# Products of low weights over the last 64 features, two at a time in half of the rows each

## The reference

```python
x = normalized_resid_pre                                   # [64, 36, 192]
q = jnp.einsum('bsd,hde->bshe', x, W_Q) + b_Q              # 12 heads of 64
k = jnp.einsum('bsd,hde->bshe', x, W_K) + b_K
v = jnp.einsum('bsd,hde->bshe', x, W_V) + b_V
scores = jnp.einsum('bqhe,bkhe->bhqk', q, k) / math.sqrt(D_HEAD)   # causal mask
pattern = jax.nn.softmax(scores, axis=-1)
z = jnp.einsum('bhqk,bkhe->bqhe', pattern, v)
attn_out = jnp.einsum('bqhe,hed->bqd', z, W_O) + b_O
```

## Time and profile before

| | |
|---|---|
| median of 3 runs | 899.01 us (897.86 to 900.95) |
| profiled execution, its time | 903.05 us |
| its span | 901.3 us |
| PE busy | 818.9 us (91%) |
| PEld busy | 733.5 us (81%) |
| DVE busy | 542.0 us (60%) |
| ACT busy | 439.9 us (49%) |
| POOL busy | 408.7 us (45%) |

### The profile page before, as it was taken

How to read it: one execution, slowest core, us unless ns; L and a number is a source line. 1 busy time by engine, 2 the same in 40 slices (tenths; PEclk the granted TensorE clock), 3 DMA queues, 4 the chain that set the end, 5 groups by cost and what they waited for, 6 DMA issues and landing times. The chain is left out here.

```text
span 901.3 us, 21350 instructions
## 1 busy us (share of the span) xinstructions
PE 818.9 (91%) x7767; PEld 733.5 (81%) x7767; DVE 542.0 (60%) x1467; ACT 439.9 (49%) x1094; POOL 408.7 (45%) x489
## 2 busy tenths in 40 slices
PE   9899999999998898987999989888879999999973
PEld 8889998899997676766999976666657899899973
DVE  2235565556665898993763337788966622467645
ACT  0246555555644576763345527566626221355523
POOL 1534444344444544342442236767841455244444
PEclk9999999999999999996999989898979999999996
DMA  9910111111110232225200013623200111333252
GB/s 308 265 51 21 31 27 37 31 32 30 37 37 2 35 67 26 34 22 172 24 1 1 1 27 50 157 47 65 46 3 2 36 60 63 81 99 107 77 170 94
DMA packets 103942, 55.78 MB, mean 62 GB/s; under 512 B 67264, under 2 KB 94512, under 8 KB 103840
## 3 DMA queue, kind: packets, MB, share of 16 engines
q1 hardware_dynamic: 99248, 45.99, 21.2%
q0 software_dynamic: 3792, 7.84, 2.5%
q10 hardware_dynamic: 800, 0.59, 0.2%
HBM read 29.81 MB, written 13.97 MB: 49 GB/s over the span
## 5 line engine op out<-in xcount | busy, mean ns | idle before, releaser
L931 POOL TENSOR_TENSOR attn_prob<-attn_prob,attn_recip 100x432 f32<-100x432 f32 x64 | 58.6, 916 | 67.1 <-DVE attn_recip L1316 66.6
L450 POOL TENSOR_TENSOR attn_prob_x<-attn_prob,attn_recip 100x864 f32<-100x864 f32 x32 | 52.6, 1644 | 52.8 <-DVE attn_recip L759 52.8
L1892 POOL DMA_INDIRECT results<-moe_hid_shared x43 | 41.1, 955 | 58.1 <-ACT moe_hid_shared L2107 58.1
L1602 ACT ACTIVATE mlp_hid<-psum,columns 128x384 f32<-128x384 f32 x72 | 38.1, 580 | 41.4 <-PE psum L96 41.4
L1047 PE MATMUL psum<-ident,attn_prob 100*108 100x100 f32 x256 | 35.5, 264 | 21.4 <-POOL attn_prob L931 12.9
L1047 PEld LDWEIGHTS psum<-ident,attn_prob 100*108 100x108 f32 x256 | 26.1, 138 | 27.2 <-POOL attn_prob L931 18.7
L1064 PEld LDWEIGHTS psum<-attn_prob_t,attn_values 108*49 108x49 f32 (+1 forms) x1024 | 33.7, 132 | 15.5 <-ACT attn_prob_t L1183 6.7
L1176 ACT ACTIVATE attn_prob<-attn_prob 100x432 f32<-100x432 f32 x64 | 36.1, 564 | 19.0 <-POOL attn_prob L938 17.8
L2082 ACT ACTIVATE moe_silu<-psum 128x384 f32<-128x384 f32 x36 | 17.7, 491 | 56.5 <-PE psum L107 56.5
L1064 PE MATMUL psum<-attn_prob_t,attn_values 108*49 108x36 f32 (+1 forms) x1024 | 36.0, 217 | 8.3 <-DMA attn_values<-attn_v_tok 5.0
L1555 PE MATMUL psum<-mlp_w_dn_s,mlp_hid 128*128 128x192 f32 (+2 forms) x306 | 42.6, 290 | 0.0
(11 more groups left out here) (474 smaller groups left out, 2790.5 us busy)
## 6 DMA issues: line engine op xcount, KB each, us to landing
embed_patches<-in_x SPq DMA_DIRECT2D x8, 768.0 KB, 14.5
sorted_rows<-mlp_pad_zeros SPq DMA_DIRECT2D x1, 4214.0 KB, 15.6
moe_hid_shared<-sorted_rows SPq DMA_DIRECT2D x43, 98.0 KB, 2.1
attn_v<-attn_v_tok SPq DMA_DIRECT2D x16, 216.0 KB
attn_values<-attn_v_tok SPq DMA_DIRECT2D x96, 27.0 KB
side_raw_a<-in_w_gu_dram SPq DMA_DIRECT2D x8, 288.0 KB, 3.2
side_raw_b<-in_w_gu_dram SPq DMA_DIRECT2D x16, 144.0 KB, 3.4
h_rows<-results SPq DMA_DIRECT2D x6, 288.0 KB, 5.4
```

The costliest lines, as they stand in the source:

```text
L450: nc.gpsimd.tensor_tensor(prob_x[k % 2][:, :, :, :], prob[k % 3][:, :, :].rearrange("p h (a n) -> p h a n", a=1) .to_broadcast([QP, HEADS, ...
L931: nc.gpsimd.tensor_tensor(pr, pr, recip[k % 2][:, :].rearrange("p (h a) -> p h a", a=1) .to_broadcast([QP, HEADS, SEQ]), ALU.mult).then_in ...
L1602: nc.scalar.activation(hid_step(n), bank(n % 3)[:, 0:MW], ACT.Gelu, bias=b_up[:, c:c + 1]).then_inc(S["gelu_done"], 1)
L1892: nc.gpsimd.indirect_dma_start(out=results, out_offset=bass.IndirectOffsetOnAxis(ap=x_in[j % x_ring][:, D:D + 1].bitcast(U32), axis=0), in ...
```

## The change

The low products of the last 64 features need only 64 rows, w_lo and x_hi. The change computes them in pairs: the query chunk's product in the upper half of the rows, the key chunk's in the lower half, and for values the left 384 columns above and the right 384 below. For the lower half x_hi must lie in partitions 64 to 127 as well, which a new tile `b_upper` holds, written by a third rounding on ACT for each group. `project` now makes queries and keys in one call: it waits for all three copies of the chunk two before, does four matmuls for the queries, four for the keys, and then the pair. `values` does four and four, and then the pair. The low weights of the first attention are subtracted over all 128 partitions, so three of four memsets fall away. What the diff takes from `part_views` and `width` is a view that was unused.

```diff
+        if self.b_upper is not None:
+            nc.scalar.activation(self.b_upper[DB:P, 0:MW], self.x_b, ACT.Copy).then_inc(S["next_rounded"], 1)
     def split(self, dve, S):
-        dve.wait_ge(S["next_rounded"], 2)
+        dve.wait_ge(S["next_rounded"], 2 if self.b_upper is None else 3)
...
-            def project(g, kind, c):
+            def project(g, c):
                 if c == 0 and g >= 1:
                     pe.wait_ge(S["x_split"], g)
-                if c >= 2 and kind == 0:
+                if c >= 2:
                     pe.wait_ge(S["q_copied"], chunks * g + c - 1)
-                elif c >= 2:
                     pe.wait_ge(S["k_low_copied"], chunks * g + c - 1)
                     pe.wait_ge(S["k_high_copied"], chunks * g + c - 1)
...
+                cols, toks = slice(c * P, (c + 1) * P), group_cols(g)
+                for w, out in ((w_q, q_bank(c)), (w_k, k_bank(c))):
+                    nc.tensor.matmul(out, w.a_hi[:, cols], a_hi[:, toks], start=True, stop=False)
+                    nc.tensor.matmul(out, w.a_hi[:, cols], a_lo[:, toks], start=False, stop=False)
+                    nc.tensor.matmul(out, w.a_lo[:, cols], a_hi[:, toks], start=False, stop=False)
+                    nc.tensor.matmul(out, w.b_hi[:, cols], b_x[:, toks], start=False, stop=False)
+                nc.tensor.matmul(q_bank(c), w_q.b_lo[0:DB, cols], b_x[0:DB, toks], start=False, stop=True
+                                 ).then_inc(S["q_done"], 1)
+                nc.tensor.matmul(k_bank(c), w_k.b_lo[DB:P, cols], b_upper[DB:P, toks], start=False, stop=True
+                                 ).then_inc(S["k_done"], 1)
...
                     nc.tensor.matmul(out, b_x[:, toks], w_v.b_hi[:, cols], start=False, stop=False)
-                    nc.tensor.matmul(out, b_x[:, toks], w_v.b_lo[:, cols], start=False, stop=True
-                                     ).then_inc(S["v_done"], 1)
+                nc.tensor.matmul(bank(0)[:, 0:half], b_x[0:DB, toks], w_v.b_lo[0:DB, 0:half], start=False, stop=True
+                                 ).then_inc(S["v_done"], 1)
+                nc.tensor.matmul(bank(1)[:, 0:half], b_upper[DB:P, toks], w_v.b_lo[DB:P, half:HID],
+                                 start=False, stop=True).then_inc(S["v_done"], 1)
...
                 nc.scalar.activation(b_x[0:DB, at], bank(1)[0:DB, 0:n], ACT.Copy).then_inc(S["x_rounded"], 1)
+                nc.scalar.activation(b_upper[DB:P, at], bank(1)[0:DB, 0:n], ACT.Copy).then_inc(S["x_rounded"], 1)
...
-                dve.wait_ge(S["x_rounded"], 2 * g)
+                dve.wait_ge(S["x_rounded"], 3 * g)
...
-                    for w in (w_q1, w_k1, w_v1, w_qkv2_split):
-                        nc.gpsimd.memset(w.b_lo[DB:P, :].bitcast(F32), 0.0).then_inc(S["pads_cleared"], 1)
+                    nc.gpsimd.memset(w_qkv2_split.b_lo[DB:P, :].bitcast(F32), 0.0).then_inc(S["pads_cleared"], 1)
```

More of the change, by code:

```diff
@@ L198, with __init__ @@
 class FirstTokens:
-    def __init__(self, nc, psum, ident, neg_half, rows_, x, banks, ready, norm=None, room=None):
+    def __init__(self, nc, psum, ident, neg_half, rows_, x, banks, ready, norm=None, room=None, b_upper=None):
         self.nc, self.ident, self.neg_half, self.rows, self.ready, self.norm = nc, ident, neg_half, rows_, ready, norm
+        self.b_upper = b_upper
         self.a_hi, self.a_lo, self.b = (t[:, 0:MW] for t in (x.a_hi, x.a_lo, x.b))
@@ L337, in keep_going, with wide_stage @@
         nc.tensor.matmul(out[:, 0:2 * D], ident[:, :], constants, start=True, stop=True)
-def wide_stage(nc, kept, small, psum, ident, neg_half, name, rings, make_following, h_tok, w_q, w_k, w_v, w_o, bias, q_bias, k_bias, out_bias):
+def wide_stage(nc, kept, small, psum, ident, neg_half, name, rings, b_upper, make_following, h_tok, w_q, w_k, w_v, w_o, bias, q_bias, k_bias, out_bias):
     groups, units = TOK // WIDE, TOK // UNIT
@@ L513, in values @@
                 at = (t % RING) * P
-                toks = slice(at, at + P)
+                toks, half = slice(at, at + P), HID // 2
                 for b in range(2):
@@ L522, in values @@
                         pe.wait_ge(S["k_high_copied"], chunks * (g + 1))
-                    cols, out = slice(b * 384, (b + 1) * 384), bank(b)[:, 0:384]
+                    cols, out = slice(b * half, (b + 1) * half), bank(b)[:, 0:half]
                     nc.tensor.matmul(out, a_hi[:, toks], w_v.a_hi[:, cols], start=True, stop=False)
@@ L588, in _ @@
             for c in range(chunks):
-                project(0, 0, c)
-                project(0, 1, c)
+                project(0, c)
             for t in new_tiles(0):
@@ L608, in _ @@
                                 odd_banks_free(k)
-                            project(g, 0, c)
-                            project(g, 1, c)
+                            project(g, c)
                     else:
@@ L2378, in split_views @@
     return [padded(t, width, pad) for t in out] if pad else out
-def part_views(src, first, n, width):
-    cols = src[:, first:first + n]
-    return cols.rearrange("p (h e) -> p h e", e=width) if width else cols
 def remainder_weight_jobs(nc, which, eng, S, stage_a, stage_b, jobs):
     for j, (_, n, parts) in enumerate(jobs):
-        for stage, view, p in ((stage_a, 0, P), (stage_b, 2, DB)):
+        for stage, view in ((stage_a, 0), (stage_b, 2)):
             eng.wait_ge(S["weight_hi_done"], 2 * j + (2 if view else 1))
-            for first, count, views, width in parts:
-                last = which.tensor_tensor(views[view + 1][0:p],
-                                           part_views(stage[j % STAGED], first, count, width)[0:p],
+            for first, count, views, low_rows in parts:
+                p = low_rows if view else P
+                last = which.tensor_tensor(views[view + 1][0:p], stage[j % STAGED][0:p, first:first + count],
                                            views[view][0:p].bitcast(F32), ALU.subtract)
@@ L2413, in round_one @@
     for stage, view in ((stage_a, 0), (stage_b, 2)):
-        for first, count, views, width in parts:
-            last = nc.scalar.activation(views[view], part_views(stage[j % STAGED], first, count, width),
-                                        ACT.Copy)
+        for first, count, views, _ in parts:
+            last = nc.scalar.activation(views[view], stage[j % STAGED][:, first:first + count], ACT.Copy)
         last.then_inc(S["weight_hi_done"], 1)
@@ L2620, in split_b @@
                                 ALU.subtract).then_inc(self.S["split"], 1)
-PADS = 4
+PADS = 1
 def build(nc, x, tok_w, tok_b, pos, wq1, wk1, wv1, w_qkv2, w_fc1, w_fc2, w_qkv3, columns_dram,
@@ L2675, in build, with plain @@
             w_q1, w_k1, w_v1 = (Split(fsb, n, HID) for n in ("w_q1", "w_k1", "w_v1"))
-            def plain(w, n):
-                return [(0, n, split_views(w, 0, n), None)]
+            b_upper = fsb("b_upper", [P, RING * P], F32R)
+            def plain(w, n, low_rows=P):
+                return [(0, n, split_views(w, 0, n), low_rows)]
             jobs = [(wq1, HID, plain(w_q1, HID)), (wk1, HID, plain(w_k1, HID)),
-                    (wv1, HID, plain(w_v1, HID)), (w_qkv2, 3 * D, plain(w_qkv2_split, 3 * D))]
+                    (wv1, HID, plain(w_v1, HID)), (w_qkv2, 3 * D, plain(w_qkv2_split, 3 * D, DB))]
             later = {}
@@ L2795, in prepare @@
                         "vector_start": vector_start, "gpsimd": gpsimd}
-            first_of_attn1 = FirstTokens(nc, psum, ident, neg_half, h_tok, rings, (6, 7), ("embedded", 3))
+            first_of_attn1 = FirstTokens(nc, psum, ident, neg_half, h_tok, rings, (6, 7), ("embedded", 3), b_upper=b_upper)
             embed_stage(nc, kept, first_of_attn1, psum, "embed", x, tok_w.rearrange("(c p) n -> p c n", p=P), pos, rows(tok_b, P),
@@ L2809, in first_of_attn2 @@
                 return FirstTokens(nc, psum, ident, neg_half, h_tok, rings, (0, 1), ("y_ready", 3), norm_cols(0), room)
-            wide_stage(nc, kept, later, psum, ident, neg_half, "attn1", rings, first_of_attn2, h_tok, w_q1, w_k1, w_v1, w_o1, bias1, q_bias1,
+            wide_stage(nc, kept, later, psum, ident, neg_half, "attn1", rings, b_upper, first_of_attn2, h_tok, w_q1, w_k1, w_v1, w_o1, bias1, q_bias1,
                        k_bias1, out_bias1)
```

## The result

| | before | after |
|---|---|---|
| median of 4 runs each, us | 899.96 (897.86 to 900.95) | 924.95 (920.89 to 928.66) |
| ratio of the times, 95% interval | | 1.028 (1.0231 to 1.0329) |
| profiled execution, us (span) | 903.05 (901.3) | 920.89 (919.2) |
| mean granted clock of it | 0.961 | 0.974 |

The change made the kernel slower by 25.0 us of the medians, where 25.1 was the forecast. So each term was read for itself.

A forecast was written before the change was run, and what follows sets the result against it. PE's matmul start distances were taken to set the pace in the first attention. Chunks 12.4 + 0.1, value tiles 8.8, transposes 3.1, ends 0.4 and rounding 0.3 gave 25.1 us on 899.0, so 924 us, range 908 to 932.

The forecast's parts named there:

- chunks of group 0: Query and key chunks of the first group: changes of form around each pair, 0.27 us net a pair; 1.6 us.
- values of group 0: Value tiles of the first group: PE waits for ACT's copy of bank 0 between tiles, and changes form; 2.0 us.
- third rounding: ACT's extra 64 x 256 copy per group delays DVE's splitting, which PE awaits in group 1; +0.3 us.
- tile to tile in the steps: Passages between value tiles of one group, where bank 0's copy loses its cover: +0.88 us each, 7.0 us.
- tile to transposes: From a group's last value tile to the next group's transposes, which wait for both copies: +0.5 us, six times, 3.1 us.
- chunks in the steps, with the turned probabilities: Query and key chunks in the pipelined steps: each pair pays entering and leaving, 0.27 us net; 10.9 us.
- end of the last group's values: After group 7's last value tile, where no transposes wait: changes of form less the saved slot, 0.2 us.
- The stages behind 290 us: Everything after the first attention: only shifted, with no stage's length changing by more than 2 us.
- without a drain: Rival: PE changes between full rows and half rows without draining; +2.5 us, 901.5 us; chance 0.13.
- With the loads made ahead: Rival: weight loads still come ahead, so each change of form pays only running out; +12 us, 911 us; chance 0.10.
- The serial pair: Rival: full drain, and the pair's two halves start 0.1 us or more apart instead of together; chance 0.12.
- Faster: Rival: no drain and a short passage after a value tile; 894 us with the copy wholly covered; chance 0.03.

The follow-up runs named there:

- third rounding only: The kernel before plus ACT's additional copy of each group, awaited by DVE's splitting and read by nothing else; median 899.33 us, ratio 1.0005.
- order only: The changed kernel's new order, but with full matmuls on zero-padded weights and no third rounding; median 910.29 us, ratio 1.0116 to the kernel before.
- two pairs in one stretch: Changed kernel with pairs for queries and keys alone, every second chunk's pair first, right behind the previous chunk's; median 902.23 us, ratio 1.0028 to the kernel before.
- both in the upper rows: Changed kernel with pairs for queries and keys alone, the key product also on partitions 0 to 63; median 918.32 us, ratio 1.0193 to the kernel before.

## Why the prediction was right, step by step

| term | predicted, us | measured, us | where |
|---|---|---|---|
| chunks of group 0 | 1.6 | 1.5 | first stretch, 2.13 less the wait below |
| wait of the values for the last query copy | none | 0.6 | end of the first stretch |
| values of group 0 | 2.0 | 2.0 | 0.78 + 0.87 + 0.23 in the second stretch, 0.1 of open load behind it |
| third rounding | 0.3 | 0.4 | group 1, and third rounding only |
| tile to tile in the steps | 7.0 | 6.7 | eight passages, 0.81 to 0.89 each |
| tile to transposes | 3.1 | 3.1 | six, 0.52 or 0.53 each (2.54 to 3.07) |
| chunks in the steps, with the turned probabilities | 10.9 | 9.0 | 21 times two chunks, 0.43 in the mean |
| output products behind a chunk | none | 0.6 | 11 x 0.06 (2.07 to 2.12 or 2.13) |
| end of the last group's values | 0.2 | 0.2 | its second tile |
| sum | 25.1 | 24.1 | of 24.24, the rest is rounding |

The measured terms are differences between the two traces, block by block. The bound, the count of passages and the mechanism held. Two terms were mis-sized, by 1.9 and 0.3 us, and two waits were missing, 0.6 us each; so the sum came out 0.9 us above the stage's 24.2.

*Chunks in the steps* were 1.9 us too dear. The prediction took 0.11 us of open load on leaving, whatever follows. Half the chunks leave to the turned probabilities (line 559), and there it hardly shows. For instance, two chunks with them took 93.65 to 97.51, 3.86 us, before, and 102.97 to 107.28, 4.31 us, after. That is +0.45, not +0.54: the first chunk +0.16 (its own open load was there already, behind the mixing), the second +0.26 (1.32 to 1.58), the turned ones +0.03 (1.12 to 1.15).

*Bank 0 of the first value tile.* The prediction followed the copies of chunks 2 to 5 against one another, and not what comes behind the last. PE's and ACT's timeline of the kernel after:

```profile
58.26 0.39 PE L510 MATMUL psum<-ring_b,w_q_b_lo 64*128 64x288 f32 x1
...
58.69 0.50 ACT L649 ACTIVATE attn_q<-psum,columns 128x288 f32<-128x288 f32 x1 [0.69 <-PE psum L510]
...
59.24 0.44 PE L528 MATMUL psum<-w_v_a_hi,ring_a_hi 128*128 128x384 f32 x1 [0.58 <-ACT attn_q L649]
```

The first tile's bank 0 is a query bank. Its copy used to run under the key matmuls; now it starts at the pair's end, and PE waits. The first value matmul comes 0.98 us behind the pair, where leaving alone takes 0.33: 0.65 us. It is the same mechanism as between two value tiles, in one more place. *The output products*, told under order only, are the other missing term.

*Tiles in the steps* came out 0.3 us under: 0.84 us a passage in the mean rather than 0.88. The kernel before took 1.84 to 1.87 us there and not the 1.76 of ten slots, for the first tile behind other work had an open load already; the kernel after took 2.68 to 2.70 and not 2.64.

Chunk 2 of group 0 went as worked out: the stage's start to its first matmul is 3.73 us (48.56 to 52.29), and 3.72 us in the kernel before to where its keys could start. GpSimd's fuller subtraction cost nothing that shows: of the kernels that have it for queries and keys, one starts the stage at 45.48 us (two pairs in one stretch) and the kernel before at 46.68.

Of what was named as a test, all held but one. The pair came 0.22 us behind the full matmul, its halves 0.00 us apart, the next 0.33 us later; idle times were 0.58 to 0.66 between tiles and 1.04 at the transposes (about 1.1 named). The stretch grew by 24.2 us (some 268 named for 243.4). The stages behind 290 us, which were to stay within 2 us, changed by 8.2: this test was set too narrow, for they vary by 9.9 us from one kernel to the next along with the granted clock.

The rivals: without a drain the pair would come 0.13 us behind the full matmul; it came 0.22 us behind. With the loads made ahead it would be 911 us and no open load at the second full matmul; the trace has 0.24 us there. The serial pair was made (both in the upper rows) and costs a further 5.2 us. Faster needed a passage behind a value tile with the copy nearly covered; order only, which has no change of form at all, was still 10.4 us slower in the stage.

## What to carry to other kernels

Before two short matmuls are joined side by side in row halves, count the changes of form and not the slots saved: here one way in and out cost 0.40 us and a pair saved 0.13 us, so by this estimate a stretch needs four pairs before it pays. Then look at what the join does to the last matmul of each accumulator: a bank that was copied under its neighbour's matmuls is now ready together with it, and the new order alone cost 10.4 us here. If the time must be split between such causes, keep the new order and put the old instructions back; and compare stages between the same two instructions, since the rest of the program varied by 9.9 us with the clock.

## What the runs showed of the hardware that was not expected

- The open weight load behind a change of form depends on what follows: 0.11 us ahead of a full matmul of 288 or 384 columns (0.24 to the next start, not 0.13), 0.03 us ahead of the 100-column turned probabilities.
- Within the 64-row form loads are made ahead again when the rows are the same: in both in the upper rows 105.96 for a matmul at 106.09. The first full matmul after it has its load at its own start, 106.31.
- Two 64-row matmuls of different row halves with loads of 128 columns each start within 0.01 us of each other, and so do their loads (both at 118.52 in the kernel after), as those with 36 columns did in the earlier trace rows.
- ACT's copy of a finished values bank began 0.38 us after the last matmul's start in the earlier trace rows, 0.46 us after it in order only, and 0.47 to 0.56 us after a pair's start, of which the pair's open load is about 0.11.
